# Four activations of the first chunk moved from ScalarE to VectorE, in units of 256 tokens

## What is computed

```
x_proj = silu(x @ W1 + b1)                  # 512 columns
u, v, q, k = split(x_proj, 4)
scores = q . k per head                     # 2048 x 2048, 16 heads
av = (silu(scores) / 2048) @ v              # per head
y = layernorm(av * u, gamma, beta) @ W2 + b2
x = layernorm(x + y)
h = silu(fp4(x) @ fp4(w_gate).T) * (fp4(x) @ fp4(w_up).T)   # 352 wide
out = layernorm(x + fp4(h) @ fp4(w_down).T)
```

## Time and profile before

| | us |
|---|---|
| median of 3 runs | 515.11 (514.42 to 515.18) |
| the profiled execution, its own time | 515.08 |
| its span, first to last instruction | 512.9 |
| TensorE matmul busy | 496.4 |
| ScalarE busy | 486.6 |
| VectorE busy | 284.7 |
| GpSimd busy | 82.0 |

### The profile page before, as it was taken

How to read it: one execution, slowest core, us unless ns; L and a number is a source line. 1 busy time by engine, 2 the same in 40 slices (tenths; PEclk the granted TensorE clock), 3 DMA queues, 4 the chain that set the end, 5 groups by cost and what they waited for, 6 DMA issues and landing times.

```text
span 512.9 us, 20251 instructions
## 1 busy us (share of the span) xinstructions
PE 496.4 (97%) x9062; PEld 262.7 (51%) x9064; DVE 284.7 (55%) x730; ACT 486.6 (95%) x547; POOL 82.0 (16%) x180
## 2 busy tenths in 40 slices
PE   8899999999999999999999999999999999999996
PEld 5453335434444444444444444444467777777762
DVE  7644934654838465573946466483844443435445
ACT  4999999999999999999999999999999999999940
POOL 8413000101020201111030111102020311112020
PEclk9999999999999999999999999999999999999999
DMA  4732450000000000000000000000000000000000
GB/s 129 190 96 61 111 147 23 1 3 2 3 6 3 8 2 8 2 8 1 3 8 3 8 1 8 1 3 7 3 8 4 9 4 10 9 4 8 4 10 10
DMA packets 15173, 11.87 MB, mean 23 GB/s; under 512 B 1815, under 2 KB 14750, under 8 KB 15086
## 3 DMA queue, kind: packets, MB, share of 16 engines
q1 hardware_dynamic: 13800, 8.85, 6.5%
q0 software_dynamic: 704, 1.33, 1.0%
q10 hardware_dynamic: 582, 0.40, 0.3%
HBM read 1.92 MB, written 1.05 MB: 6 GB/s over the span
## 4 chain that ended last, share of the span: by engine, by line
PE 57%; ACT 29%; issue 9%; DVE 3%; DMA 1%; POOL 0%; POOLq 0%; SPq 0%; DVEq 0%
PE ps L451 55%; ACT attn L713 29%; PE ps L465 2%; DMA q_stack<-parts 1%; DMA gate_b<-in_L_attn_b 0%; ACT feat L713 0%; ACT v_sb L713 0%; POOL rstd_b L417 0%; DVE parts L823 0%; DVE xn_b L850 0%; DVE stats_b L880 0%; DVE magic_b L1012 0%; DVE xn_b L854 0%; DVE xn_b L856 0%; DVE xn_b L858 0%
## 5 line engine op out<-in xcount | busy, mean ns | idle before, releaser
L713 ACT ACTIVATE attn<-ps 128x1024 f32<-128x1024 f32 x512 | 474.6, 1307 | 1.2 <-PE ps L451 0.9
L451 PE MATMUL ps<-attn,v_pad 128*32 128x256 f32 (+1 forms) x5120 | 274.4, 341 | 0.3 <-DVE wdown_t L1079 0.2
L451 PE MATMUL ps<-q_stack,k_stack 64*128 64x256 bf16 (+1 forms) x2560 | 172.4, 251 | 9.1 <-ACT attn L713 1.3
L451 PEld LDWEIGHTS ps<-attn,v_pad 128*32 128x32 f32 x5120 | 132.2, 109 | 80.3 <-issue 38.8
L451 PEld LDWEIGHTS ps<-q_stack,k_stack 64*128 64x128 bf16 x2560 | 77.7, 94 | 128.3 <-ACT attn L713 80.6
L416 POOL TENSOR_TENSOR ve_a<-mv_a,eps_col 128x1 f32<-128x1 f32 x24 | 4.6, 190 | 207.4 <-DVE mv_a L882 207.4
L416 POOL TENSOR_TENSOR ve_b<-mv_b,eps_col 128x1 f32<-128x1 f32 x24 | 4.5, 190 | 193.5 <-DVE mv_b L882 193.5
L880 DVE BATCH_NORM_STATS2 stats_b<-ps 128x6 f32<-128x128 f32 x9 | 2.7, 298 | 31.7 <-PE ps L451 31.7
L880 DVE BATCH_NORM_STATS2 stats_a<-ps 128x6 f32<-128x128 f32 x8 | 2.4, 299 | 26.3 <-PE ps L451 26.3
L942 DVE COPY xqT<-ps 128x128 f32<-128x128 f32 x15 | 4.4, 292 | 22.2 <-PE ps L451 22.2
L451 PE MATMUL ps<-zeros 128*128 128x512 bf16 x49 | 13.8, 424 | 1.4 <-DVE zeros L1006 1.2
(11 more groups left out here) (189 smaller groups left out, 408.5 us busy)
## 6 DMA issues: line engine op xcount, KB each, us to landing
q_stack<-parts SPq DMA_DIRECT2D x18, 128.0 KB, 2.4
k_stack<-parts SPq DMA_DIRECT2D x12, 128.0 KB, 3.1
k_stack<-parts SPq DMA_DIRECT2D x15, 64.0 KB, 2.6
x_sb<-in_L_attn_x SPq DMA_DIRECT2D x3, 256.0 KB, 4.3
q_stack<-zeros SPq DMA_DIRECT2D x6, 128.0 KB, 2.5
k_stack<-parts POOLq DMA_DIRECT2D x9, 64.0 KB, 2.6
q_stack<-parts SPq DMA_DIRECT2D x8, 64.0 KB, 2.0
out<-x_a SPq DMA_DIRECT2D x8, 64.0 KB, 1.5
```

Source lines behind the costliest of these rows:

```text
L451: return pe.matmul(to, lhsT, rhs, start=start, stop=stop, skip_group_check=True)
L713: return act.activation(to, frm, ACT.Silu, **kw)
```

## The change

Three activations of the first chunk are done by VectorE: k from token 1792 on (256 tokens), u of the first 512 tokens and q of 256 to 511. u's job of 512 columns becomes two of 256 (early_u 0 and 256), so that there are four units of one shape. Each unit is a chain of 13 operations on VectorE, activate_early. The job of k 1792 moves from step 7 to step 5, v 3 from step 9 to step 8, the two u units are at 9 and 12, q 256 stays at 14. In VectorE's order zero_v(3) moves ahead of the split of k 1280, activate_early of k 1792 follows that split, and the two u units and q with its split come ahead of the weights' quantisation. The four units are taken out of ACT_JOBS, so TensorE waits for VectorE to have read their banks; split waits for no semaphore for k 1792 and q 256, whose silu is now on its own engine.

```diff
-    PREP_AT = {0: ("v", 1), 2: ("xT", 1280), 3: ("xT", 1792), 4: ("k", 1280), 6: ("v", 2), 7: ("k", 1792), 9: ("v", 3),
-               12: ("u", 0), 14: ("q", 256), 16: ("u", 1), 18: ("q", 512), 20: ("u", 2), 22: ("q", 1024),
-               24: ("u", 3), 26: ("q", 1536), 29: ("w2", 0), 31: ("gate", 0), 32: ("up", 0), 33: ("down", 0)}
+    PREP_AT = {0: ("v", 1), 2: ("xT", 1280), 3: ("xT", 1792), 4: ("k", 1280), 5: ("k", 1792), 6: ("v", 2), 8: ("v", 3),
+               9: ("early_u", 0), 12: ("early_u", 256), 14: ("q", 256), 16: ("u", 1), 18: ("q", 512), 20: ("u", 2),
+               22: ("q", 1024), 24: ("u", 3), 26: ("q", 1536), 29: ("w2", 0), 31: ("gate", 0), 32: ("up", 0),
+               33: ("down", 0)}
+
+    EARLY = (("k", 1792), ("early_u", 0), ("early_u", 256), ("q", 256))
...
-                if kind in ("k", "q", "v", "u") or (kind == "gate" and tile is not None and tile not in BY_VEC)]
+                if kind in ("k", "q", "v", "u") and (kind, i) not in EARLY or (kind == "gate" and tile is not None and tile not in BY_VEC)]
...
+                elif kind == "early_u":
+                    last = project(bank, "u", i, LW)
...
-                else:
+                elif (kind, start) not in EARLY:
                     dve.wait_ge(job_by_act, ACT_JOBS.index(job_no[(kind, start, None)]) + 1)
...
+            def activate_early(kind, start):
+                r = ROWS[1]
+                x, n, f = r.gate[:, 0:LW], r.magic[:, 0:LW], r.xn[:, 0:LW]
+                spare = r.hqT[:, :, :].rearrange("p t n -> p (t n)")[:, 0:LW]
+                col = ("early_u", "q", "k").index(kind)
+                to = uT[:, start:start + LW] if kind == "early_u" else feat[:, unit_no[(kind, start)] % FEAT, 0:LW]
+                bank = wait_made(kind, start, None)
+                dve.tensor_scalar(x, ps[:, bank, 0:LW], b1_col[:, col:col + 1], X_MIN,
+                                  ALU.add, ALU.max).then_inc(job_by_vec, 1)
+                wait_taken(kind, start, None)
+                link(dve.tensor_scalar(n, x, -LOG2_E, Y_MIN, ALU.mult, ALU.max))
+                link(dve.tensor_scalar(spare, n, ROUND, None, ALU.add))
+                link(dve.scalar_tensor_tensor(out=f, in0=spare, scalar=ROUND, in1=n,
+                                              op0=ALU.subtract, op1=ALU.subtract))
+                link(dve.tensor_scalar(n.bitcast(U32), spare.bitcast(U32), 23, None, ALU.logical_shift_left))
+                link(dve.scalar_tensor_tensor(out=spare, in0=f, scalar=POWERS[4] / LAST, in1=f, op0=ALU.add, op1=ALU.mult))
+                for power in (3, 2, 1):
+                    link(dve.scalar_tensor_tensor(out=spare, in0=spare, scalar=POWERS[power] / LAST, in1=f,
+                                                  op0=ALU.add, op1=ALU.mult))
+                link(dve.scalar_tensor_tensor(out=spare, in0=spare, scalar=POWERS[0] / LAST, in1=n,
+                                              op0=ALU.add, op1=ALU.mult))
+                link(dve.tensor_scalar(spare, spare, LAST, 1.0, ALU.mult, ALU.add))
+                link(dve.reciprocal(f, spare))
+                link(dve.tensor_tensor(to, x, f, ALU.mult))
...
             zero_v(2)
+            zero_v(3)
             split("k", 1280)
-            zero_v(3)
+            activate_early("k", 1792)
...
             split("k", 1792)
+            activate_early("early_u", 0)
+            activate_early("early_u", 256)
+            activate_early("q", 256)
+            split("q", 256)
             dve.wait_ge(w_loaded, 16 * W_LOADS)
             quantise_rows(wgate_n)
-            split("q", 256)
             quantise_rows(wup_n)
```

More of the change, by code:

```diff
@@ L30 @@
 Y_MAX, Y_MIN = 120.0, -125.0
+X_MIN = -Y_MAX / LOG2_E
 POWERS = (1.00000007, -0.69314697, 0.2402212, -0.05550713, 0.00967554, -0.00132765)
@@ L127, in build @@
             PARTS_AT |= {first: (t - 1, (0, 1)), first + 1: (t - 1, (2,))}
+    LW = 256
     JOB_AT = {at: (kind, i, None) for at, (kind, i) in PREP_AT.items()}
@@ L761, in job @@
                 act.wait_ge(job_made, k + 1)
-                if (kind, i) == ("u", 0):
+                if kind == "u":
                     act.wait_ge(b1_ready, 2)
```

## The result

The changed kernel takes 518.40 us (median of 6 runs, 518.23 to 521.09), the kernel before 514.87 (6 runs, 513.88 to 515.26). The ratio is 1.0086, 95% interval 1.0072 to 1.0101: slower. The ratio is larger than that of the medians (1.0069), because two of the six executions, 520.49 and 521.09 us, had a mean granted clock of 0.993 where the others had 0.996 to 0.998.

What follows compares the result with a forecast made beforehand. ScalarE was taken as the bound (42.60 to 72.10 us); it loses 1.29 us of work, but two stalls behind VectorE leave step 17 3.06 us late: 515.08 + 3.06 = 518.1 us. Range 517.2 to 519.0 (55%), outer 516.6 to 520.4.

Steps and rivals of the forecast that it cites:

- the prediction's signs: ScalarE idle in the first chunk: about 1.9 us ahead of step 7's first half, 2.1 us ahead of step 17's.
- 17a: First half of ScalarE's step 17 (a, b: a step's halves); forecast at 52.82 against 49.76, 3.06 us late.
- The price of a unit: VectorE's chain of 13 operations on 256 tokens: 6.79 us each, bounds 6.6 to 7.0, 27 us in all.
- the errata rule: Skill's fixed latency of 58 cycles per VectorE operation: 5.7 us a unit by estimate; rejected from the profile's rows.
- the flush rule: Skill's flush of duration minus 266 ns behind each VectorE operation: 9.2 us a unit, some 7 us later; rejected.
- The first wait: v 2's job waits for VectorE's first operation on k 1792 until 29.23; ScalarE's step 7 at 30.9 instead of 28.8.
- The second wait: TensorE's job 16 (u 1) waits from about 49.0 until VectorE reads q's bank; starts 51.41, step 17 3.06 us late.
- What else is queued: VectorE's later splits, quantisations and w2 job, and k 1792's transfers: all claimed hidden, w2 result taken at 80.7.
- The clock rival: In the second stall TensorE's clock falls to 0.50: 519 to 521 us, value 520; chance 20%.
- only the first stall: Rival: q's first operation comes by 48.8, so no second stall, needing units of 5.94 us; 515.6 us, chance 7%.
- VectorE keeps ahead: Rival: both stalls vanish with units under some 5.8 us, leaving ScalarE's 1.29 us saving; 513.8 us, chance 4%.
- hidden, by 1.6 us: Gate weights' job behind w2: VectorE done with w2 at 81.2, TensorE begins the job at 82.8, so no wait.

Runs made afterwards that it cites:

- e10: Changed kernel with only the splits of q 1024 and q 1536 moved behind the first tile's copy of hqT; 518.20 us, ratio 1.0082 to the kernel before.
- e4: Changed kernel with 20 TensorE matmuls of zeros put ahead of the wait of job 16 (u 1); 518.25 us, ratio 1.0065 to the kernel before.
- e7: Changed kernel with three unused memsets of 512 columns on VectorE between u 256 and q 256, lengthening the wait; 521.70 us, ratio 1.0137.
- e1: Changed kernel with VectorE reading k 1792's bank before the split of k 1280 instead of behind it; 518.28 us, ratio 1.0068.
- e3: Changed kernel with both early reads: k 1792's bank before the split of k 1280, q 256's within u 256's chain; 516.86 us, ratio 1.0040.
- e8: Changed kernel with only k 1792 on VectorE, u 0 and q 256 back on ScalarE; 515.81 us, ratio 1.0021 to the kernel before.
- e2: Changed kernel with VectorE reading q 256's bank within u 256's chain, into its own buffer; 517.23 us, ratio 1.0049 to the kernel before.
- e5: e3 with the splits of q 1024 and q 1536 moved behind the first tile's copy of hqT; 514.79 us, ratio 1.0003 to the kernel before.
- e9: Changed kernel with k 1792 back on ScalarE, jobs from step 9 not in neighbouring steps, splits of q 512, 1024, 1536 later; 514.14 us, 0.9983 to kernel before.

## Why the prediction was right, point by point

Forecast 518.1 us, measured 518.40; the mechanism is checked step by step here.

**ScalarE is the bound, and its saved work is worth nothing while it waits.** Right. The 1.29 us came off it, and waits of 1.69 and 2.7 us (e10, e4; 3.76 with the clock down) took their place; the prediction's signs had 1.9 and 2.1. The 2.1 does not follow from its own times: 17a at 52.82 less the end of 16b at 50.26 is 2.56.

**The price of a unit, 6.79 us.** Nearly. From one first operation to the next step of the list the four took 6.83 (29.14 to 35.97), 7.10 (37.78 to 44.88), 6.84 (44.88 to 51.72) and 6.84 (51.72 to 58.56). The first operation takes 0.48, not the 0.42 of a plain copy from PSUM; the reciprocal took the 1.75 interpolated. Together the units ahead of q's read make it 0.4 us later than forecast: this is the term that was too small. Most of it is u 0, where two one-tensor operations took 0.36 and 0.49 us (at 38.63 and 42.11) instead of 0.29; u 0 takes 7.09 to 7.12 in e4, e7 and e10 too, but 6.83 in e1 and e3. Why is open. The unit of k 1792 adds nothing, as u 0 waits 0.28 us for its bank behind it; for that reason the prediction's bounds of 2.5 and 3.7 us, which let three units count, should have been 2.7 and 3.5. The two other prices named in the prediction, estimates from the Trainium skill (VectorE: DVE Perf Modes, sections "The TRN2 errata — SBUF-src ops pay a fixed extra latency per instruction" and "The DRAIN you can't avoid"), 5.7 us by the errata rule and 9.2 by the flush rule, are both off in this trace.

**The first wait.** Right: v 2 was forecast to start at 29.23, and started at 29.67 in an execution that ran 0.47 late. e8 shows it alone, e1 shows that it does not count beside the second.

**The second wait.** Right in place and cause: TensorE's wait of 2.4 us was 2.54, 17a 3.06 us late was some 3.5. In e10, without the fall of the clock, 17a starts at 52.02 in an execution in which k 1280 was read at 24.30, 1.20 earlier than before: 52.02 + 1.20 less 49.76 is 3.46. The medians differ by 3.53. The difference to the forecast is the 0.4 us of the units.

**What else is queued is hidden.** Right for this kernel. In the profile VectorE even waits 1.68 us for the w2 bank, but there the fallen clock had delayed that bank. In e4, whose edit leaves VectorE's list as it is and where the clock held, VectorE reads w2 without waiting at 81.00 (forecast 80.7), and TensorE's gate and up jobs do not wait for it:

```profile
81.00 0.28 DVE L1107 TENSOR_TENSOR w_centred<-w_gamma,ps 128x128 f32<-128x128 f32 x1
```

Taking 4.5 us off the list ahead of it changes nothing (e10). The transfers of k 1792's parts held nobody up either; no wait for them stands in TensorE's timeline of the changed kernel. In e1, where TensorE comes there sooner, it waited 1.22 us for them; in e3, where it comes as early, it did not, so the order of the jobs alone does not decide it.

**The clock rival.** It had 20% and a price of 519 to 521. It is no alternative to the forecast but a thing that befalls some executions: two of six here, at 520.5 and 521.1; the median is without it. By the prediction's own sign (wrong if the clock leaves 1.00 near 51 us) the profiled execution belongs to this rival and not to the forecast; had one or two more executions been like it, the median would have too.

**The two rivals without the second wait.** They were 515.6 (only the first stall) and 513.8 (VectorE keeps ahead), and both need cheaper units, which no run tried. e2 and e3 take the second wait away at the full price of the units, and lie at 517.2 and 516.9. There the list that the prediction calls "hidden, by 1.6 us" is the next bound: the 1.6 leans on the 3.06 us of the second wait, and without it VectorE is 1.46 us late for the gate job; in e3 that job waited 1.41. With cheaper units the list would be shorter as well, so 515.6 is not refuted by these runs. 513.8 counts all of ScalarE's saving as won; e5, with neither the second wait nor the late list, is at 514.8 and loses the saving to smaller waits. A stall that hides another is to be priced with the other behind it.

## What to carry to other kernels

Moving work from a bound engine to one that is half idle helped here only where the idle time lay ahead of the places where others wait for that engine. Walk its list in order with start times, up to every read that frees a bank or a buffer, and look at the next such read when one wait is removed. Release the shared buffer first and calculate later, and put what is needed late (here two splits not needed until 96 steps or more behind the first chunk) behind the crowded stretch. Then the same move, with the part that cannot be made early left where it was, gave 0.17% (e9).

## What the runs showed of the hardware beyond that

TensorE's granted clock fell to its 1.2 GHz level in a single standstill of 2.5 us within a kernel that otherwise holds it at 1.00, in some executions and not in others (in e10's profiled execution it held 1.00 through a standstill of 2.53 us), and it stayed low well beyond the standstill: in the profile of the changed kernel its mean was 0.78 in the microsecond from 51, 0.50 from 52 and still 0.81 in the one from 58, while TensorE worked again from 52.26. That cost 2.2 to 2.8 us (520.5 and 521.1 against 518.3), about as much as the standstill itself; in the traces the stretch from k 1280's read to q 512's read takes 35.37 us with the fall and 32.85 in e4 without it, 2.5 more. 20 matmuls of zeros into a bank in use kept it at 1.00 (e4).
